# Feature-pair tower on one core: the last K-tile of layer 1 becomes a rounded one-pass contraction, and the first four K-tiles grow from 117 to 128 rows

## The reference

```
x1[b,s,d] = relu(sum over h,m of W1[s,h,m] * e[b,h,d] * e[b,m,d] + b1[s])      (128 outputs s)
x2[b,s,d] = relu(sum over h,m of W2[s,h,m] * x1[b,h,d] * e[b,m,d] + b2[s])
z = concat(x1.sum(d), x2.sum(d), dense_ctx)
y = relu(relu(z @ W_top1 + b_top1) @ W_top2 + b_top2) @ W_top3
```

## Time and profile before

| | us |
|---|---|
| median of 3 runs (lowest, highest) | 1186.08 (1184.38, 1195.46) |
| profiled execution | 1195.75 |
| its span (first to last instruction) | 1193.7 |
| PE busy | 1110.4 (93%) |
| DVE busy | 946.2 (79%) |
| POOL busy | 842.8 (71%) |
| ACT busy | 801.2 (67%) |

### The profile page before, as it was taken

The page is one execution under the profiler, slowest core; times in us unless marked ns, Lnnn a source line. Parts: engine busy times, 40 slices in busy tenths (PEclk is TensorE's granted clock), DMA queues, the critical chain, the costliest instruction groups (busy, mean ns, idle before and its releaser), DMA issues.

```text
span 1193.7 us, 17611 instructions
## 1 busy us (share of the span) xinstructions
PE 1110.4 (93%) x4507; PEld 830.7 (70%) x4507; DVE 946.2 (79%) x2860; ACT 801.2 (67%) x2718; POOL 842.8 (71%) x951
## 2 busy tenths in 40 slices
PE   0059999999999999999999999999999999999998
PEld 0027777777777777777777667777777777777687
DVE  4027888889898989898888668888888888886787
ACT  5016767777777767777777567777677777775674
POOL 6754787788687887788688646887877884453354
PEclk9999999999999999999999999999999999999999
DMA  6256568764876568674876428765676757763342
GB/s 178 37 125 141 110 126 174 153 137 88 178 165 125 117 131 184 135 149 87 183 163 124 98 49 180 164 134 106 130 176 144 147 97 175 168 130 78 66 86 48
DMA packets 73708, 154.70 MB, mean 130 GB/s; under 512 B 14435, under 2 KB 27637, under 8 KB 73606
## 3 DMA queue, kind: packets, MB, share of 16 engines
q0 software_dynamic: 28272, 85.81, 40.6%
q1 hardware_dynamic: 45334, 67.77, 21.4%
HBM read 66.49 MB, written 3.81 MB: 59 GB/s over the span
## 4 chain that ended last, share of the span: by engine, by line
PE 81%; DVE 6%; issue 5%; DMA 2%; ACT 2%; SPq 2%; another core or an unknown queue 1%; DVEq 0%; ACTq 0%
PE bank L682 63%; PE l_acc L666 15%; DVE acc L548 3%; DMA z<-e_rows 2%; ACT prod L421 1%; PE misc L715 1%; PE misc L711 1%; DVE z L508 1%; DVE p2acc L566 0%; DMA e_rows<-e_t 0%; DVE t_sum L556 0%; DVE p L589 0%; DVE t_sum L560 0%; DVE p2l L602 0%
## 5 line engine op out<-in xcount | busy, mean ns | idle before, releaser
L421 ACT ACTIVATE prod<-bank,emb 128x128 f32<-128x128 f32 x2552 | 720.5, 376 | 305.5 <-PE bank L682 272.4
L548 DVE SCALAR_TENSOR_TENSOR acc<-bank,emb,acc 128x128 f32<-128x128 f32 x2184 | 613.3, 340 | 142.7 <-PE bank L682 124.7
L682 PE MATMUL bank<-w2h,x1h 128*128 128x512 f32 (+1 forms) x1280 | 535.4, 418 | 9.4 <-DVE acc L548 6.1
L682 PE MATMUL bank<-w2l,x1h 128*128 128x512 f32 (+1 forms) x1280 | 494.3, 386 | 0.0
L682 PE MATMUL bank<-w2h,x1l 128*128 128x512 f32 (+1 forms) x1280 | 467.0, 427 | 5.5 <-issue 3.8
L310 POOL DMA_INDIRECT emb<-tbl,idx x312 | 310.5, 995 | 82.2 <-issue 76.0
L682 PEld LDWEIGHTS bank<-w2h,x1h 128*128 128x128 f32 x1280 | 240.8, 188 | 107.6 <-issue 56.9
L682 PEld LDWEIGHTS bank<-w2h,x1l 128*128 128x128 f32 x1280 | 240.5, 188 | 89.8 <-issue 35.7
L330 POOL TENSOR_TENSOR tree<-prod 128x640 f32<-128x640 f32 x127 | 240.2, 1892 | 83.2 <-DMA prod<-prod 83.2
L682 PEld LDWEIGHTS bank<-w2l,x1h 128*128 128x128 f32 x1280 | 240.7, 188 | 61.5 <-issue 22.4
L321 POOL DMA_DIRECT2D prod<-prod x127 | 125.1, 985 | 173.7 <-ACT prod L421 171.5
(11 more groups left out here) (96 smaller groups left out, 289.3 us busy)
## 6 DMA issues: line engine op xcount, KB each, us to landing
prod<-prod POOLq DMA_DIRECT2D x127, 640.0 KB
z<-e_rows SPq DMA_DIRECT2D x160, 234.0 KB
z<-e_rows SPq DMA_DIRECT2D x192, 78.0 KB
emb<-tbl,idx POOLq DMA_INDIRECT x312
z<-e_rows SPq DMA_DIRECT2D x32, 156.0 KB
prod<-w_by_h SPq DMA_DIRECT2D x3, 832.0 KB
e_rows<-e_t SPq DMA_DIRECT2D x8, 256.0 KB
wt<-w_top SPq DMA_DIRECT2D x2, 512.0 KB
```

The costliest lines, as they stand in the source:

```text
L421: last = nc.scalar.activation(prod[:, ct % P_RING, i, n * S:(n + 1) * S], bank[:, (ct * NB + k) % RING, n * S:(n + 1) * S], ACT.Copy, scal ...
L548: nc.vector.scalar_tensor_tensor(dst, src, scale, dst if step else b2_row[:, :], ALU.mult, ALU.add).then_inc(v_step, 1)
L682: last = nc.tensor.matmul(out_bank[:, 0:b - a], x, w[:, a:b], start=(n == 0), stop=(n == 2))
```

## The change

Each of the first four K-tiles takes 11 more pairs (shift 18 + t, h below 11) on the rows 117 to 127. That leaves 10 + 7 + 9 + 8 = 34 pairs of the shifts 18 and 19 (`REST_RANGES`; shift 20 is folded in by the symmetry as before), which form the tile REST. REST has no unshifted rows in PSUM: both factors are loaded, each row three times, one factor into the tile `rest` (`load_rest_first`, 4 DMAs), the other into slot 6 of `z` (4 DMAs at the end of `load_shifted`). DVE multiplies the two into `z` (L595), ACT rounds the product to float32r into `rest` (`round_rest`, L486), DVE turns the three copies into minus high, low and minus high (`mix_rest`, L606), and PE contracts the 102 rows with `w_rest`, which holds minus high, high and minus low weights, in one float32r matmul. `w_rest` is made once. The other K-tiles keep float32. The order of making and contracting changes too: from chunk 1 on REST is made first (g = 1) and contracted fourth (g = 18), the others are made one place later, and the first contraction stands at g = 10 where it stood at 7; in chunk 0 REST is last. `y` becomes a row of `h2`.

```diff
-Z_GROUPS = (range(0, 1), range(1, 4), range(4, 7))
+REST = NF - 1
+Z_GROUPS = (range(0, 1), range(1, 4), range(4, REST))
+EXTRA = P - KP * M
+EXTRA_TILES = 4
+REST_RANGES = ((18, 11, 21), (18, 32, 39), (19, 11, 20), (19, 31, 39))
+N_REST = sum(b - a for _, a, b in REST_RANGES)
+F_ROWS = [P] * EXTRA_TILES + [KP * M] * (REST - EXTRA_TILES) + [3 * N_REST]
...
-CONTRACT_AT = (7, 10, 13, 16, 19, 22, 25)
+FIRST_CONTRACT_AT = (7, 10, 13, 16, 19, 22, 25)
+CONTRACT_AT = (10, 13, 16, 18, 19, 22, 25)
+CONTRACT_ORDER = (0, 1, 2, REST, 3, 4, 5)
...
+def made_before(f, t):
+
+    if f == 0:
+        return t
+    return 0 if t == REST else t + 1
+
+
+def round_at(f):
+    return 20 if f == 0 else 6
+
+
+def mix_at(f):
+    return 21 if f == 0 else 11
...
+            def rest_rows(f, row, n):
+                tile, q = divmod(f, CPT)
+                return bass.AP(tensor=e_rows[tile % 2], offset=row * ROW + q * CH, ap=[[ROW, n], [0, 3], [1, CH]])
+
+            def load_rest_first(f):
+                sp.wait_ge(et_stored[f // CPT % 2], 64 * (f // CPT // 2 + 1))
+                wait(sp, f_used, NF * f)
+                at = 0
+                for _, a, b in REST_RANGES:
+                    sp.dma_start(rest[3 * at:3 * (at + b - a), :].bitcast(F32), rest_rows(f, a, b - a)
+                                 ).then_inc(in_first, 16)
+                    at += b - a
...
+                sp.dma_start(z[KP * M:P, r, NF, :], rows(0, [[ROW, EXTRA], [1, CH]])).then_inc(in_rep[r], 16)
                 for k, ts in enumerate(Z_GROUPS):
+                    a, b = ts[0], ts[-1] + 1
                     for h in range(KP):
...
+                        sp.dma_start(z[h * M:(h + 1) * M, r, a:b, :],
+                                     rows(KP * a + h, [[ROW, M], [KP * ROW, b - a], [1, CH]])).then_inc(in_z[r][k], 16)
+                    if a < EXTRA_TILES:
+                        sp.dma_start(z[KP * M:P, r, a:b, :],
+                                     rows(KP * REST + a, [[ROW, EXTRA], [ROW, b - a], [1, CH]])).then_inc(in_z[r][k], 16)
+                at = 0
+                for k, a, b in REST_RANGES:
+                    sp.dma_start(z[3 * at:3 * (at + b - a), r, REST, :], rest_rows(f, a + k, b - a)
+                                 ).then_inc(in_second[r], 16)
+                    at += b - a
...
             for f in range(CHUNKS):
+                if f > 1:
+                    load_rest_first(f - 1)
                 if f % CPT == 0:
                     store_rows(f // CPT)
                 load_shifted(f)
+                if f == 0:
+                    load_rest_first(0)
...
+            load_rest_first(CHUNKS - 1)
...
+            def round_rest(f):
+                act.wait_ge(f_made, NF * f + made_before(f, REST) + 1)
+                nc.scalar.copy(rest[0:3 * N_REST, :], z[0:3 * N_REST, f % 2, REST, :]).then_inc(rest_high, 1)
...
+                if t == REST:
+                    dve.wait_ge(in_first, 64 * (f + 1))
+                    dve.wait_ge(in_second[f % 2], 64 * (f // 2 + 1))
+                    nc.vector.tensor_tensor(part, rest[0:rows, :].bitcast(F32), part, ALU.mult).then_inc(f_made, 1)
+                    return
...
+            def mix_rest(f):
+                rows = F_ROWS[REST]
+                dve.wait_ge(rest_high, f + 1)
+                nc.vector.scalar_tensor_tensor(rest[0:rows, :], z[0:rows, f % 2, REST, :], marks[0:rows, 0:1],
+                                               rest[0:rows, :].bitcast(F32), ALU.mult, ALU.subtract
+                                               ).then_inc(rest_mixed, 1)
...
+                if t == REST:
+                    pe.wait_ge(w_rest_mixed, 1)
+                    pe.wait_ge(rest_mixed, f + 1)
+                    w, x = w_rest[0:rows, :], rest[0:rows, :]
+                else:
+                    pe.wait_ge(f_made, NF * f + made_before(f, t) + 1)
+                    w, x = w1[0:rows, t, :], z[0:rows, f % 2, t, :]
```

More of the change, by code:

```diff
@@ L77, with pairs @@
 E_SLOTS = 3
+def made_before(f, t):
[6 more added lines that the diff above has]
+    return 21 if f == 0 else 11
+def pairs(t):
+    if t == REST:
+        rest = [(h, (h + k) % M) for k, a, b in REST_RANGES for h in range(a, b)]
+        return [(3 * i + c, h, m) for c in range(3) for i, (h, m) in enumerate(rest)]
+    rows = [(k * M + h, h, (h + KP * t + k) % M) for k in range(KP) for h in range(M)]
+    if t < EXTRA_TILES:
+        rows += [(KP * M + h, h, (h + KP * REST + t) % M) for h in range(EXTRA)]
+    return rows
 def pair_weights(w1):
@@ L84, in pair_weights, with rest_marks @@
     for t in range(NF):
[L85 to L90, removed]
-    return ahead, back
+        for p, h, m in pairs(t):
+            ahead[p, t] = w1[:, h, m]
+            if m != h:
+                back[p, t] = w1[:, m, h]
+    return ahead, back
+def rest_marks():
+    marks = np.zeros((P, 3), np.float32)
+    for c, values in enumerate(((0, 1, 0), (1, -1, 0), (0, -1, -1))):
+        marks[c:3 * N_REST:3] = values
+    return marks
 def build(nc, dram, tables, out):
@@ L123, in build @@
         z = sb("z", [P, 2, NF + 1, CH])
+        rest = sb("rest", [P, CH], F32R)
+        w_rest = sb("w_rest", [P, S], F32R)
         x1h = sb("x1h", [P, 2, CH], F32R)
@@ L379, in _ @@
             nc.scalar.copy(back_stage, w1_back).then_inc(back_staged, 1)
+            act.wait_ge(in_marks, 16)
+            act.wait_ge(w1_summed, 1)
+            nc.scalar.activation(w_rest[:, :], w1[:, REST, :], ACT.Copy, scale=marks[:, 1:2]).then_inc(w_rest_high, 1)
             for k, (a, b) in enumerate(W2_PIECES):
@@ L472, in _ @@
                 for g in range(GB):
+                    if f < CHUNKS and g == round_at(f):
+                        round_rest(f)
                     if f < CHUNKS and g == X1_AT:
@@ L496, in _ @@
                                     ).then_inc(w1_summed, 1)
+            dve.wait_ge(w_rest_high, 1)
+            nc.vector.scalar_tensor_tensor(w_rest[:, :], w1[:, REST, :], marks[:, 2:3], w_rest[:, :].bitcast(F32),
+                                           ALU.mult, ALU.subtract).then_inc(w_rest_mixed, 1)
             for k, (a, b) in enumerate(W2_PIECES):
@@ L503, in make_f @@
                 rows = F_ROWS[t]
+                part = z[0:rows, f % 2, t, :]
+                if t == REST:
[3 more added lines that the diff above has]
+                    return
                 dve.wait_ge(rep_ready, f + 1)
@@ L626, in _ @@
                     if f < CHUNKS and g in MAKE_AT:
-                        make_f(f, MAKE_AT.index(g))
+                        make_f(f, [t for t in range(NF) if made_before(f, t) == MAKE_AT.index(g)][0])
+                    if f < CHUNKS and g == mix_at(f):
+                        mix_rest(f)
                     if f < CHUNKS and g == X1L_AT:
@@ L665, in contract @@
                     wait(pe, x1l_done, f)
-                nc.tensor.matmul(l1_acc[:, :], w1[0:rows, t, :], z[0:rows, f % 2, t, :],
-                                 start=(t == 0), stop=(t == NF - 1)).then_inc(f_used, 1)
+                if t == REST:
+                    pe.wait_ge(w_rest_mixed, 1)
[4 more added lines that the diff above has]
+                    w, x = w1[0:rows, t, :], z[0:rows, f % 2, t, :]
+                nc.tensor.matmul(l1_acc[:, :], w, x, start=(turn == 0), stop=(turn == NF - 1)).then_inc(f_used, 1)
             def layer2_bank(c, j, k):
```

52 lines of the change are left out of this document (28 added, 24 removed).

## The result

| | before, beside these runs | after |
|---|---|---|
| median us (lowest, highest) | 1187.34 (1184.38, 1195.46) | 1246.66 (1244.31, 1248.23) |
| profiled execution, its span | | 1247.47, 1245.7 |

After over before is 1.050, with a 95% interval of 1.048 to 1.053: 59 us slower, where the forecast was no change and the range ended at 1209.

A forecast was written before the change was run, and what follows sets the result against it. The prediction took PE to bound the kernel and summed -19.5 (gain) + 9.5 (new-tile loads) + 8 (start) + 5 (POOL) = +3 us, giving 1189 us, range 1168 to 1209.

The forecast's parts named there:

- PE as the bound: Steady part: PE, busy 99.86 of 100 us, sets the pace, with a period of 32.86 us a chunk.
- the 19.5: Gain in us: one of seven contractions falls from 0.86 to 0.23 us, saving 0.63 in each of 31 chunks.
- SP's pace: At a new tile SP issues loads at 0.74 us each, the 23rd about 17 us after the first.
- The stop at bank 8: At new tiles DVE's wait delays scaling of bank 3, so PE stalls 1.4 us at layer-2 bank 8.
- The costs set at nothing: Rounding on ACT and mixing on DVE at g = 11 cost nothing, at most 0.6 us a chunk.
- The start: Chunks 0 and 1: exposed loads delay DVE's first product in chunk 1 by 1 to 11 us, taken as 8.
- So REST's second factor lands at 591 to 595 us: New tiles: landing 1.5 to 5.5 us after issue, taken as 593.1, so DVE waits 2.3 us.
- a forecast of 9.5: PE's total loss in us from late REST loads: 1.4 us at each of seven new tiles; bounds 0 and 26.
- the loads of REST are late: Rival: DVE waits for the last of 23 DMAs at new tiles and start; 1208.6 us, chance 0.20.
- that is so in 8 of 31 chunks: REST's product at g = 1 meets POOL's addition L330 in 8 chunks, stalling PE 0.6 us each, 5 us.
- the rival 18.6: Rival: REST's product meets POOL's addition in every chunk, 18.6 us instead of 5; 1203 us, chance 0.07.
- the bound of 10 us: Upper bound of the loss from POOL blocking REST's product, if it takes the worst 2.4 us.

The follow-up runs named there:

- e7_gain18: Kernel before, seventh contraction one float32r pass on constant tiles at g = 18, the change's contraction places, no added loads, rounding or mixing: 1171.67 us, 0.987 of before.
- e9_hold: Changed kernel, SP holding the next chunk's loads back at each new tile after the first until DVE has made REST's product: 1245.68 us.
- e10_spread: Changed kernel, REST's eight loads reshaped to 16, 16, 1 and 1 source rows per factor, same bytes and DMA count: 1234.89 us, 1.041 of before.
- e2_psum: Changed kernel, REST's product and mixing taking one input from PSUM from chunk 1 on (wrong numbers), load order kept: 1226.63 us, 1.034 of before.
- e1_loads: Changed kernel, REST's loads right behind the first K-tile group, the first factor's only at new tiles: 1205.02 us, 1.015 of before.
- e3_both: Changed kernel with REST's loads moved forward as in e1_loads and one input in PSUM as in e2_psum: 1179.95 us, 0.994 of before.
- e5_place: Changed kernel, same load order, REST made third (g = 7), rounded at 12, mixed at 17, contracted fifth (g = 21): 1191.71 us, 1.002 of before.
- e4_gain: Kernel before, seventh contraction one float32r pass on constant tiles at g = 25, no added loads, rounding or mixing: 1179.62 us, 0.993 of before.

## Why the prediction was wrong

**What was right.** PE as the bound, 32.86 us a chunk and its fall to 32.24: after has it where nothing interferes, and e7_gain18 shows 15.8 (by the ratio) to 17.6 us (by the medians) of the 19.5 as time. SP's pace: 17.9 us for 23 issues against 17.0. The stop at bank 8, through DVE's queue. The costs set at nothing: L606 has a median of 744 ns (longest 1901), and DVE waited for `round_rest` once, 0.7 us.

**What came out by luck.** The start: +8 forecast, 7.4 + 1.8 = 9.2 measured. The 8 was counted from rows of an execution in which SP took 28 us for 24 issues and DVE had a hole of 10 us; the second profile of before has 15.5 us and no hole. The prediction put the product of chunk 1 at 1 to 11 us behind 89.61, and said that without the hole the loss would be up to 9 us more. In after it starts at 88.62, ahead of 89.61, and in the second profile of before at 79.48. So SP's pace and the hole, both wrong, cancelled.

**What failed first: "So REST's second factor lands at 591 to 595 us".** The step took a landing lag of 1.5 to 5.5 us from the first loads of a train, with none of SP's own ahead of them, and gave it to the last of 23. DVE's waits at the seven new tiles were 2.8 to 9.2 us, 38.2 in all, where I had 7 x 2.3 = 16; the upper bound of 4.6 us each, 32, was too low too. Bytes alone would not have said it, since 2.2 MB at 110 GB/s are 20 us, as late as my 17.0 + 3.5. What I had not asked is how full the engines are: 87% busy, with POOL's queue for 47.5%, so that, by this reading, the last load waits behind what the fullest engine still holds (e9_hold: not behind later ones, and at c = 7 with 1.6 of 16 engines busy in the last 2.6 us; e10_spread: the loads' shapes are some 8 us of 43). The trace of before could have said it. The row of busy times by stretch for its same stage, from the first issue to DVE's first product, has a DMA share of 0.90:

```profile
572.62:590.79 18.17, 17.61 (x75) 13.48 (x74) 16.18 (x52) 14.38 (x50) 13.86 (x16) 1.00 0.90 187
```

To this comes a term that was missing: half clock behind most of the stalls. Together the seven chunks cost 42.8 us beside a forecast of 9.5, and 47 with the gain that they don't show. The rival "the loads of REST are late" was the right mechanism with too small a price, at most 26.

**What failed second: "that is so in 8 of 31 chunks".** I read where POOL's L330 stood in before and took it to stay there. In after, away from the new tiles, POOL's addition starts within 0.6 us of the product in most chunks; the product has a median of 2407 ns, and e2_psum makes the price 20 us (1246.66 to 1226.63) where the sum had 5 and the rival 18.6. I gave that rival 0.07, on the argument that DVE's and POOL's places both follow PE. They don't quite: POOL's addition waits for the accumulating DMA, and in after, e1_loads and e3_both it stands beside g = 1, while before and e7_gain18, with the change's contraction places but before's loads, have it 2 to 6 us away in three chunks of four. So the contraction places are not what moved POOL. It may be the loads, or the added rounding and mixing; no run parts these, and the path is open. POOL's total wait for that DMA fell from 83 and 94 us in the two profiles of before to 66 in after, but only to 79 in e3_both.

The Trainium skill's rule in "SBUF — State Buffer", section "Who interferes with whom", holds in these runs in that the two contend, with 2.4 us against 0.68, and with one input in PSUM the block is gone (671 to 693 ns). That the second to issue is the blocked one is not what the starts show: DVE's came 0.3 us first at 261.42, and DVE was blocked. What the rule could not tell is when the two meet; that was mine to bound, and the bound of 10 us was too low by half.

Both errors meet at one place: a new instruction stood at g = 1, where its loads were needed earliest and PE's slack behind it was some 1 us. In e5_place the same work, with the product at g = 7 and the first contraction back at g = 7, costs 55 us less.

## What to carry to other kernels

The issue of the last load in a train says little of its landing where the DMA engines are some 87% busy: take the landing lag from a load at the same place of a train, and issue what is needed first before the bulk. A stall of PE can cost more than its own length, since the clock can fall with it. Before adding a product with both inputs in SBUF, ask at which step the other engine's large addition can stand, not where it stands now; put the product where it can slip, or keep one input in PSUM. A saving on the bound engine can be lost where the next engine is tight: the same 0.6 us a chunk gave 15.8 us in e7_gain18 and 8 in e4_gain.

## What the runs showed of the hardware

- At the PE stalls of 2.7 to 8.3 us in chunk 0 and six of the new tiles of after the granted clock was 0.5 (1.2 GHz) for 3.4 to 10.2 us, in the longer ones partly within the stall; one stall of 3.06 us (c = 19) had no such stretch. In the stretch from 336.00 to 346.50 it was 0.51 and PE busy for 6.01 us.
- The product that POOL blocked had itself started first by the profile: DVE at 261.42, POOL at 261.71, and it took 2.85 us where 0.68 is usual. POOL's addition took 2.00, no more than the 2.01 beside the product of e2_psum or the median of 1.97 in before. So having started first did not protect DVE's instruction, and POOL's shows no delay.
- A DMA share near 0.1 does not mean that the loads have landed: in e9_hold it was 0.10 for the last 2.6 us of an 8.30 us wait for one.
- A single profiled execution can carry a pause that others don't: 42.21 us and 32.94 us for the same chunk 0 of the same kernel, with 24 issues of SP ahead of it in 28 us and in 15.5 us. Rows from a program's start want a second profile before a sum rests on them.
